# One decoder layer on one core: the attention stage's steps put into another order on four engines

## The chip, the cores and the metric

The kernel runs on one core of a Trainium2 chip. The metric is the device time of that core in microseconds (us), from the start of one execution to its end; a profiled execution also gives the span from the first to the last instruction.

## What is computed

Inputs are `x` and `ctx`, 16 sequences of 128 rows of 128 float32 values. Three sublayers follow each other, each with a residual and a layer norm:

```python
x = _layernorm(x + attention(x))            # 16 heads of 8, rotary q and k, softmax over 128 keys
x = _layernorm(x + cross(x, ctx))           # q, k, v = (. @ Wq + bq); correlation by FFT, mean over
                                            # batch and channels, top 11 lags, softmax, rolled sum of v
x = gamma * norm(x + moe(x)) + beta         # 8 experts, top 2 of a gate, relu(x W1 + b1) W2 + b2
x = _layernorm(x)                           # the layer's own norm behind the last sublayer's
# attention, per sequence: qkv = x @ w_qkv.T; q, k = rope(q), rope(k)
# softmax(q @ k.T * 8 ** -0.5) @ v, then @ w_out.T + b_out
```

The change lies in the first sublayer only. All products are carried to float32 accuracy.

## The kernel before

**The stages.** The attention stage fills the first 103 us or so, a short serial stage finds the lags of the cross attention, and from about 115 us on the experts run until the end. Nothing behind the attention stage's last steps is edited.

**One sequence through the attention stage.** The stage works on the sequences n = 0 to 15 one after the other, in a software pipeline; each sequence passes these steps, each a small helper that waits for its semaphores and issues one or a few instructions on one engine:

- TensorE: `qkv(n)` (L953) projects x and the context. `k_transposes(n)` (L1006) and, for n below 3, `q_transposes(n)` (L1014) turn the stacked pieces. `scores(n, u)` (L968), u = 0 and 1, gives two halves of the scores, from which only row maxima are taken. `maxima_transpose(n)` (L1024) turns the maxima into rows. `scoresT(n, u)` (L985) gives the transposed scores with the maxima already subtracted. `weighted(n, u)` (L1030) multiplies the exponentials by v and by ones. `project(n)` (L1052) is the output projection. `keep_clock(n)` and `keep_clock_late(...)` issue idle matmuls, `fold_cross_query()` two small ones.
- ScalarE: `keep_qkv(n)` (L704) copies the projections out of PSUM. `first_piece(n)` (L708) writes the bf16 high parts of q and k; `second_piece(n)` and `second_copy(n)` (L721, L725) the next parts. `kT_copy(n)` (L729) copies the turned k. `mT_copy(n)` (L741) copies the turned maxima. `softmax_exp(n, u)` (L734) takes the exponentials; the four `w1_high_piece(i)` (L699) prepare the experts' first weights.
- GpSimd (POOL): `rope_products(n)` and `rope_sum(n)` (L428, L440) rotate q and k. `remainder(n)` (L446) and `third_piece(n)` (L453) form what is left behind the first and the second part. `pad_v(n)` (L499), `small_columns(n)` (L509), `inverse_deviation(n)` (L490), later `expand_v(g)` and `w1_low_piece(i)`.
- VectorE (DVE): `maxima(n, u)` (L1381) reduces the scores to row maxima, `pieces_of_maxima(n)` (L459) splits them in two bf16 pieces. `reciprocal(n)` and `divide(n)` (L1392, L1398) normalise. `residual(g)` (L1410) adds the bias to four sequences' rows of x. `residual_sum(n)`, `statistics_of_rows(n)`, `mean_and_variance(n)` and `normal_rows(n)` (L1403, L1418, L1423, L467) are the layer norm. For n below 2 DVE also does the rope steps; `keep_turned()` and `keep_folded()` copy small tiles.
- The DMA queue that SyncE issues (SP) brings the inputs, and for each sequence two kinds of transfer. `spread_maxima(n)` (L343) copies the maxima's rows from `mT` into `qT`, two transfers of 32 KB; `scoresT(n, 0)` waits for both. `q_transpose(n)` (L336), n from 3, is a transposing transfer of q's stack into `qT`; it waits for `second_copy(n)` and `third_piece(n)`, and `scores(n, 0)` and `first_piece(n + 2)` wait for it.

**What sets the order.** The order on each engine is written out by hand, as calls in program order; a step blocks everything behind it on its engine. For the middle of the stage a loop `for k in range(8, 16)` stands on each of the four compute engines (L559, L801, L1161, L1485), so that each pass, here called block k, handles for instance `qkv(k)`, `scores(k - 4, .)` and `scoresT(k - 6, .)`. SP's order is written out as well and is the same all the way: `spread_maxima(n)`, `background_load(n)`, `q_transpose(n + 3)`. The background loads with something in them are n = 4 (512 KB of inputs), 5 (tables) and 6 to 9 (a quarter of w1 each, 256 KB), and 15 (w2).

TensorE's block before the change reads:

```python
for k in range(8, 16):
    scoresT(k - 6, 0)
    scores(k - 4, 0)
    qkv(k)
    project(k - 7)
    scoresT(k - 6, 1)
    scores(k - 4, 1)
    weighted(k - 6, 0)
    weighted(k - 6, 1)
    k_transposes(k - 2)
    maxima_transpose(k - 4)
```

**Buffers that tie the engines together.** There is one `scoreT_pair` in PSUM, so `scoresT(n, 1)` waits for `softmax_exp(n, 0)`; one `score_pair`, so each `scores` waits for the `maxima` in front of it; one `rowmax` and one `mstack`; one bank for `qkv`, one for the turned k, one (`pv_bank`) for `weighted`, which is free when `divide` of the sequence in front is done.

## Time and profile before

| | us |
| --- | --- |
| median of 3 runs | 231.09 (230.35 to 231.51) |
| the profiled execution | 231.02 |
| its span, first to last instruction | 229.2 |
| TensorE busy over the span | 214.5 (94%) |
| VectorE busy | 180.9 (79%) |
| ScalarE busy | 142.5 (62%) |
| GpSimd busy | 111.2 (49%) |
| mean granted clock of TensorE | 0.994 of 2.4 GHz |

All times below count from the start of the span. PE is TensorE's matmuls, PEld its weight loads, ACT ScalarE, POOL GpSimd, SPq the queue that issues DMAs. A matmul row with x8 runs from the start of the first to the modelled end of the last; as they are pipelined, the distance from one row's start to the next one's is what the step costs, and that is how such rows are read here. The same holds for short DVE, ACT and POOL instructions, whose rows overlap by up to 0.1 us.

### The profile page before, as it was taken

The numbers are of one execution on the slowest core, as the hardware profiler recorded it, in microseconds if no ns is written. First come the engines' busy times: TensorE is split into PE (matmuls) and PEld (weight loads), VectorE is DVE, ScalarE is ACT, GpSimd is POOL, SyncE is SP. The second block draws the span as 40 slices with busy tenths as digits, with TensorE's granted clock in tenths as the row PEclk, the third lists the DMA queues.
The fourth block names the chain that finished last, engine by engine and source line by source line (L and its number), as shares of the span: only waits on it lengthen the run. The fifth ranks groups of instructions, "written<-read, shape, count | busy, mean of one in ns | idle before, by whom it ended". The sixth has DMA issues, their size and how long they took to land.

```text
span 229.2 us, 7213 instructions
## 1 busy us (share of the span) xinstructions
PE 214.5 (94%) x2724; PEld 184.1 (80%) x2724; DVE 180.9 (79%) x622; ACT 142.5 (62%) x248; POOL 111.2 (49%) x219
## 2 busy tenths in 40 slices
PE   7989899999999979999999999999999999999970
PEld 7766677787777667778887999789988999889970
DVE  0588999999899899876755779897798868875885
ACT  2487899999999995674489300991029610596112
POOL 5189879999989995513630400252002600040484
PEclk9999999999999999999999999999999999999997
DMA  5951634665655651420000000001000100001001
GB/s 138 286 134 35 106 59 65 158 135 106 149 122 91 43 92 18 127 74 1 3 0 0 3 0 1 0 4 45 4 0 0 46 3 1 0 4 46 1 16 34
DMA packets 32454, 12.32 MB, mean 54 GB/s; under 512 B 19906, under 2 KB 32290, under 8 KB 32418
## 3 DMA queue, kind: packets, MB, share of 16 engines
q1 hardware_dynamic: 31554, 11.48, 24.1%
q8 instruction: 22, 0.36, 0.7%
q10 hardware_dynamic: 864, 0.36, 0.7%
q14 instruction: 14, 0.11, 0.2%
HBM read 6.33 MB, written 1.05 MB: 32 GB/s over the span
## 4 chain that ended last, share of the span: by engine, by line
PE 79%; DMA 7%; DVE 6%; ACT 3%; issue 2%; SPq 1%; DVEq 0%; ACTq 0%
PE bank L1328 13%; PE scoreT_pair L1328 12%; PE score_pair L1298 11%; PE scoreT_pair L1298 8%; PE bank L1042 6%; PE bank L1046 5%; PE bank L965 4%; PE scoreT_pair L997 4%; PE score_pair L981 3%; DMA qT_all<-mT 2%; PE bank L1003 2%; PE bank L1059 2%; DMA early<-in_ctxT 2%; DMA qT_all<-stack 2%; PE scoreT_pair L945 2%
## 5 line engine op out<-in xcount | busy, mean ns | idle before, releaser
L1385 DVE TENSOR_REDUCE rowmax<-score_pair 128x8 f32<-128x1024 f32 x32 | 39.0, 1218 | 4.4 <-PE score_pair L981 3.5
L608 POOL TENSOR_TENSOR ve<-mv,table 128x4 f32<-128x4 f32 (+1 forms) x12 | 3.3, 275 | 78.1 <-DVE mv L1745 60.2
L737 ACT ACTIVATE early<-scoreT_pair 128x1024 f32<-128x1024 f32 x32 | 32.8, 1026 | 6.3 <-PE scoreT_pair L997 6.1
L1328 PE MATMUL bank<-w,early 128*128 128x128 f32 x256 | 30.1, 276 | 0.0
L1328 PE MATMUL scoreT_pair<-w,early 128*128 128x128 f32 x256 | 29.9, 275 | 0.0
L1328 PEld LDWEIGHTS bank<-w,early 128*128 128x128 f32 x256 | 29.5, 192 | 0.3
L1328 PEld LDWEIGHTS scoreT_pair<-w,early 128*128 128x128 f32 x256 | 29.2, 192 | 0.0
L1298 PE MATMUL score_pair<-x2T_part,w_part 128*128 128x512 f32 x108 | 28.4, 398 | 0.0
L880 ACT ACTIVATE early<-score_pair,b 128x512 f32<-128x512 f32 x38 | 25.9, 690 | 3.2 <-PE score_pair L1298 2.6
L1042 PE MATMUL bank<-early,v_pad 128*32 128x128 f32 x512 | 26.5, 279 | 0.4 <-DVE attnT L1401 0.3
L1046 PE MATMUL bank<-early,head_ones 128*32 128x128 f32 x512 | 25.8, 273 | 0.0
L1298 PEld LDWEIGHTS score_pair<-x2T_part,w_part 128*128 128x128 f32 x108 | 19.5, 188 | 5.0 <-ACT early L880 1.4
L1298 PE MATMUL scoreT_pair<-x2T_part,w_part 128*128 128x512 f32 x78 | 19.9, 391 | 0.0
L1396 DVE RECIPROCAL rden<-bank 128x128 f32<-128x128 f32 x16 | 15.3, 955 | 3.6 <-PE bank L1046 3.5
L880 ACT ACTIVATE early<-scoreT_pair,b 128x512 f32<-128x512 f32 x26 | 17.6, 690 | 0.0
L1298 PEld LDWEIGHTS scoreT_pair<-x2T_part,w_part 128*128 128x128 f32 x78 | 14.6, 188 | 3.1
L732 ACT ACTIVATE kT_all<-bank 128x1024 bf16<-128x1024 bf16 x16 | 16.3, 1020 | 0.2 <-PE bank L1003 0.2
L1042 PEld LDWEIGHTS bank<-early,v_pad 128*32 128x32 f32 x512 | 12.8, 109 | 4.5 <-ACT early L737 1.7
L1046 PEld LDWEIGHTS bank<-early,head_ones 128*32 128x32 f32 x512 | 15.4, 110 | 0.0
L1733 DVE SCALAR_TENSOR_TENSOR x_ext<-bank,gate,x_ext 128x128 f32<-128x128 f32 x32 | 11.1, 346 | 4.8 <-PE bank L1328 4.7
L997 PE MATMUL scoreT_pair<-qT_all,kT_all 64*128 64x128 bf16 x256 | 12.7, 218 | 1.8 <-DMA qT_all<-mT 1.1
L1733 DVE SCALAR_TENSOR_TENSOR x_ext<-scoreT_pair,gate,x_ext 128x128 f32<-128x128 f32 x32 | 11.1, 346 | 4.0 <-PE scoreT_pair L1328 3.7
(229 smaller groups left out, 472.3 us busy)
## 6 DMA issues: line engine op xcount, KB each, us to landing
w<-in_w SPq DMA_DIRECT2D x8, 256.0 KB, 3.7
x_ext<-in_x SPq DMA_DIRECT2D x4, 256.0 KB, 5.6
qT_all<-mT SPq DMA_DIRECT2D x32, 32.0 KB, 2.3
early<-in_xT SPq DMA_DIRECT2D x3, 256.0 KB, 4.8
early<-in_ctxT SPq DMA_DIRECT2D x3, 256.0 KB, 5.4
out<-qkv_all SPq DMA_DIRECT2D x3, 256.0 KB, 2.3
table<-in_tables SPq DMA_DIRECT2D x1, 321.0 KB
qT_all<-stack SPq DMA_TRANSPOSE x13, 3.3
```

The costliest lines, as they stand in the source:

```text
L732: act.activation(kT[n % DEEP][:, :, :], turned_slots, ACT.Copy).then_inc(s["k_T"], 1)
L737: act.activation(prob[n % 2][:, 2 * u:2 * u + 2, :, :], scoreT_pair[:, :].rearrange("p (i j s) -> p i j s", i=2, j=QUAD), ACT.Exp, scale=S ...
L880: act.activation(hT[:, c, :], hidden_bank(g, c)[:, :], ACT.Relu, bias=b1[:, c:c + 1])\
L965: pe.matmul(qkv_bank[:, 0:3 * D + XC], xT[:, n, :], wqkv[:, :], start=True, stop=True)
L997: mm = pe.matmul(scoreT_pair[:, (QUAD * side + j) * S:(QUAD * side + j + 1) * S], kT[n % DEEP][rows, 2 * j + u, :], qT[n % DEEP][rows, 2 * ...
L1042: pe.matmul(sum_bank(n)[WIDE * j:WIDE * (j + 1), 0:S], v_pad[n % 2][:, j, i, :], prob[n % 2][:, i, j, :], start=(i == 0), stop=(i == QUAD ...
L1046: mm = pe.matmul(sum_bank(n)[WIDE * j:WIDE * (j + 1), S:2 * S], head_ones[:, i * WIDE:(i + 1) * WIDE], prob[n % 2][:, i, j, :], start=Fals ...
L1298: mm = pe.matmul(hidden_bank(g, c)[:, :], w1_part[:, w, c * P:(c + 1) * P], x2T_part[:, x, :], start=(k == 0), stop=(k == 2))
L1328: mm = pe.matmul(expert_bank[k % 4][:, e4 * D:(e4 + 1) * D], hT[:, f, n * P:(n + 1) * P], w2[:, f, :], start=(c == 0), stop=(c == CH - 1))
L1385: dve.tensor_reduce(rowmax[:, H // 2 * u:H // 2 * (u + 1)], score_pair[:, :].rearrange("p (r t) -> p r t", t=S), AX_X, ALU.max).then_inc(s ...
L1396: dve.reciprocal(rden[:, :], sum_bank(n)[:, S:2 * S]).then_inc(s["rden_ready"], 1)
L1733: dve.scalar_tensor_tensor(total, product, weight, total, ALU.mult, ALU.add).then_inc(s["summed"], 1)
```

## The change

The steps are the same, each is issued once as before, and no helper is edited. What differs is the order of the calls on TensorE, ScalarE, GpSimd and VectorE from about 10 us on. The loops over k are written out. SP's order is not edited.

```diff
             # GpSimd
             rope_sum(pool, 3)
-            pad_v(1)
             third_piece(pool, 2)
             remainder(pool, 3)
             rope_products(pool, 4)
+            third_piece(pool, 3)
             rope_sum(pool, 4)
-            third_piece(pool, 3)
+            small_columns(0)
+            rope_products(pool, 5)
             remainder(pool, 4)
-            rope_products(pool, 5)
             third_piece(pool, 4)
...
-            for k in range(8, 16):
-                rope_sum(pool, k - 1)
-                third_piece(pool, k - 2)
-                small_columns(k - 4)
-                inverse_deviation(k - 8)
-                remainder(pool, k - 1)
-                rope_products(pool, k)
-                pad_v(k - 4)
+            pad_v(5)
+            remainder(pool, 9)
+            small_columns(9)
+            rope_products(pool, 10)
+            pad_v(6)
+            rope_sum(pool, 10)
+            third_piece(pool, 9)
+            inverse_deviation(2)
+            remainder(pool, 10)
...
+            remainder(pool, 11)
+            rope_products(pool, 12)
+            third_piece(pool, 11)
...
+            remainder(pool, 13)
+            rope_products(pool, 14)
+            third_piece(pool, 13)
+            pad_v(10)
+            small_columns(13)
+            rope_sum(pool, 14)
+            remainder(pool, 14)
+            rope_products(pool, 15)
             rope_sum(pool, 15)
             third_piece(pool, 14)
...
+            w1_low_piece(2)
             inverse_deviation(11)
             inverse_deviation(12)
-            pad_v(15)
             inverse_deviation(13)
+            w1_low_piece(3)
             inverse_deviation(14)
             # ScalarE
             first_piece(3)
+            keep_qkv(5)
             mT_copy(0)
-            keep_qkv(5)
+            second_piece(3)
             kT_copy(2)
-            second_piece(3)
             second_copy(3)
+            keep_qkv(6)
             first_piece(4)
             softmax_exp(0, 0)
             mT_copy(1)
             second_piece(4)
-            second_copy(4)
             softmax_exp(0, 1)
             kT_copy(3)
-            keep_qkv(6)
+            second_copy(4)
...
-            for k in range(8, 16):
-                softmax_exp(k - 6, 0)
-                second_piece(k - 2)
-                second_copy(k - 2)
-                softmax_exp(k - 6, 1)
-                kT_copy(k - 3)
-                first_piece(k - 1)
-                keep_qkv(k)
-                mT_copy(k - 4)
...
+            softmax_exp(6, 0)
+            mT_copy(7)
+            second_copy(10)
+            second_piece(10)
+            keep_qkv(12)
+            softmax_exp(6, 1)
+            kT_copy(9)
+            first_piece(11)
...
-            w1_high_piece(0)
-            w1_high_piece(1)
-            w1_high_piece(2)
-            w1_high_piece(3)
             mT_copy(13)
             softmax_exp(12, 0)
             kT_copy(15)
+            w1_high_piece(0)
             softmax_exp(12, 1)
+            w1_high_piece(1)
...
             softmax_exp(14, 0)
+            w1_high_piece(2)
             softmax_exp(14, 1)
             softmax_exp(15, 0)
             softmax_exp(15, 1)
+            w1_high_piece(3)
             # TensorE
             scores(0, 0)
+            fold_cross_query()
             k_transposes(1)
             q_transposes(1)
-            fold_cross_query()
             scores(0, 1)
...
+            k_transposes(3)
+            maxima_transpose(1)
             scoresT(0, 0)
             scores(2, 0)
-            maxima_transpose(1)
-            k_transposes(3)
+            qkv(7)
             scoresT(0, 1)
             scores(2, 1)
             weighted(0, 0)
             weighted(0, 1)
-            k_transposes(4)
             maxima_transpose(2)
             scoresT(1, 0)
             scores(3, 0)
-            qkv(7)
+            k_transposes(4)
             project(0)
             scoresT(1, 1)
             scores(3, 1)
             weighted(1, 0)
             weighted(1, 1)
+            scoresT(2, 0)
+            scores(4, 0)
+            maxima_transpose(3)
             k_transposes(5)
-            maxima_transpose(3)
-            for k in range(8, 16):
...
+            scores(8, 0)
+            scoresT(6, 0)
+            k_transposes(9)
+            maxima_transpose(7)
+            qkv(12)
+            project(5)
+            scoresT(6, 1)
+            scores(8, 1)
+            weighted(6, 0)
+            weighted(6, 1)
...
+            maxima_transpose(11)
             scoresT(10, 0)
             scores(12, 0)
             keep_clock_late(2, qkv_bank, "qkv_kept")
+            k_transposes(13)
...
             # VectorE
             third_piece(dve, 0)
+            keep_turned()
+            remainder(dve, 1)
             residual(0)
-            remainder(dve, 1)
             qT_copy(0)
-            keep_turned()
             third_piece(dve, 1)
...
             maxima(2, 1)
-            residual(2)
             pieces_of_maxima(dve, 2)
             reciprocal(0)
             divide(0)
             maxima(3, 0)
-            residual(3)
+            residual(2)
             residual_sum(0)
             maxima(3, 1)
...
+            maxima(6, 0)
+            normal_rows(dve, 0)
+            residual_sum(3)
+            maxima(6, 1)
+            residual(3)
+            pieces_of_maxima(dve, 6)
+            reciprocal(4)
+            divide(4)
+            maxima(7, 0)
...
```

In TensorE's new order block k opens with `scoresT` and then `scores` for k = 8, 10 and 14, the other way round for k = 9, 11, 12, 13 and 15; `maxima_transpose(k - 5)` and `k_transposes(k - 3)` follow behind these two, and then `qkv(k)` (in block 13 `k_transposes(10)` stands behind `qkv(13)`). On ScalarE `mT_copy(n)` for n = 5 to 10 stands directly behind `softmax_exp(n - 1, 0)`; for n = 3 and 4 it stands in front of `softmax_exp(n - 1, 0)`. The two `second` steps, in either order, and `keep_qkv(k)` then stand in front of `softmax_exp(k - 6, 1)`, with `second_copy` behind it in a few blocks.

## Rows read from the trace of the kernel before

**Rows 1.** Busy time by stretch: per engine us and (instructions), then clock, DMA share, GB/s.

```profile
10.00:20.00 10.00, 9.08 (x101) 7.14 (x99) 8.29 (x16) 7.92 (x16) 7.92 (x14) 1.00 0.55 131
20.00:30.00 10.00, 8.32 (x151) 6.23 (x152) 8.58 (x14) 8.53 (x15) 8.73 (x18) 1.00 0.47 75
...
40.00:50.00 10.00, 10.00 (x223) 7.86 (x223) 9.20 (x21) 9.53 (x17) 9.04 (x21) 1.00 0.70 160
...
80.00:90.00 10.00, 8.56 (x210) 6.58 (x208) 9.07 (x20) 8.18 (x13) 7.44 (x11) 1.00 0.34 60
```

**Rows 2.** The waits of 33.3 to 73.3 us: total us, times, longest.

```profile
DVE rden L1396 <- PE bank L1046: 2.0, 8, 0.3
ACT early L737 <- PE scoreT_pair L997: 1.9, 8, 0.2
```

**Rows 3.** The chain that ended last, 22 to 29 us: start, us, what.

```profile
22.48 0.41 PE scoreT_pair L997 x8
...
22.92 1.02 ACT early L737
...
24.14 0.60 SPq L348
...
24.78 3.53 DMA qT_all<-mT
...
28.35 0.40 PE scoreT_pair L997 x8
```

**Rows 4.** Timeline of TensorE where block 8 begins: start us, us, instruction.

```profile
32.74 0.62 PE L1003 MATMUL bank<-ident,stack 128*128 128x128 bf16 x8
33.20 0.22 PE L1028 MATMUL bank<-ident,mstack 128*128 128x128 bf16 x1
33.35 0.40 PE L997 MATMUL scoreT_pair<-qT_all,kT_all 64*128 64x128 bf16 x8
33.59 0.39 PE L981 MATMUL score_pair<-kT_all,qT_all 48*128 48x128 bf16 x8
33.91 0.93 PE L965 MATMUL bank<-wqkv,early 128*128 128x392 f32 x2
```

**Rows 5.** Timeline of TensorE around `maxima_transpose(1)`.

```profile
22.70 0.41 PE L981 MATMUL score_pair<-kT_all,qT_all 48*128 48x128 bf16 x8
23.04 0.23 PE L1028 MATMUL bank<-ident,mstack 128*128 128x128 bf16 x1
23.11 0.61 PE L1003 MATMUL bank<-ident,stack 128*128 128x128 bf16 x8
```

**Rows 6.** Timeline of ScalarE: `kT_copy(3)`.

```profile
25.51 1.03 ACT L732 ACTIVATE kT_all<-bank 128x1024 bf16<-128x1024 bf16 x1
```

**Rows 7.** `spread_maxima(7)` on SP (53.8 to 55.5 us), its landing; landing of `spread_maxima(5)`.

```profile
53.93 1.25 SPq L348 DMA_DIRECT2D qT_all<-mT  x2
...
DMA to landing us min/median/max: 2.5/2.8/3.1
...
DMA to landing us min/median/max: 2.4/2.6/2.8
```

**Rows 8.** Timeline of VectorE: `residual(2)`.

```profile
26.14 0.72 DVE L1415 TENSOR_TENSOR x_ext<-x_ext,bias 128x512 f32<-128x512 f32 x1
```

**Rows 9.** Timeline of GpSimd: `third_piece(4)`.

```profile
24.56 1.06 POOL L456 TENSOR_TENSOR stack<-rest,stack 128x256 bf16<-128x256 f32 x1
```

**Rows 10.** The tile mstack, whole run: duration ns min/median/max, first and last start.

```profile
L465 DVE TENSOR_TENSOR mstack<-rowmax,mstack x16: 194/197/332, 18.6 to 90.0; 128x16 bf16<-128x16 f32 x16
```

**Rows 11.** Timeline of SP: `q_transpose(4)`.

```profile
25.70 2.01 SPq L341 DMA_TRANSPOSE qT_all<-stack  x1
```

**Rows 12.** The chain that ended last, 77 to 86 us.

```profile
77.16 4.73 DMA qT_all<-stack
...
84.84 1.03 ACT kT_all L732
```

**Rows 13.** Timeline of GpSimd in front of `third_piece(14)`.

```profile
75.46 0.30 POOL L506 COPY v_pad<-qkv_all 128x128 f32<-128x128 f32 x1
```

More of the change, by code:

```diff
@@ new lines, in _ @@
+            first_piece(7)
+            mT_copy(4)
+            softmax_exp(3, 0)
+            second_piece(7)
+            keep_qkv(9)
+            softmax_exp(3, 1)
+            second_copy(7)
+            kT_copy(6)
+            first_piece(8)
+            softmax_exp(4, 0)
+            mT_copy(5)
+            second_copy(8)
+            second_piece(8)
+            keep_qkv(10)
+            softmax_exp(4, 1)
+            kT_copy(7)
+            first_piece(9)
+            softmax_exp(5, 0)
@@ new lines, in _ @@
+            keep_qkv(13)
+            second_copy(11)
+            softmax_exp(7, 1)
+            kT_copy(10)
+            first_piece(12)
+            softmax_exp(8, 0)
+            mT_copy(9)
+            second_copy(12)
+            second_piece(12)
+            keep_qkv(14)
+            softmax_exp(8, 1)
+            kT_copy(11)
+            first_piece(13)
+            softmax_exp(9, 0)
+            mT_copy(10)
+            second_piece(13)
+            second_copy(13)
+            keep_qkv(15)
@@ L1158, in _ @@
             weighted(1, 1)
+            scoresT(2, 0)
+            scores(4, 0)
+            maxima_transpose(3)
             k_transposes(5)
[L1160 to L1171 removed]
+            qkv(8)
@@ new lines, in _ @@
+            project(1)
+            scoresT(2, 1)
+            scores(4, 1)
+            weighted(2, 0)
+            weighted(2, 1)
+            scores(5, 0)
+            scoresT(3, 0)
+            maxima_transpose(4)
+            k_transposes(6)
+            qkv(9)
+            scoresT(3, 1)
+            scores(5, 1)
+            project(2)
+            weighted(3, 0)
+            weighted(3, 1)
+            scoresT(4, 0)
+            scores(6, 0)
+            k_transposes(7)
+            maxima_transpose(5)
@@ new lines, in _ @@
+            qkv(10)
+            project(3)
+            scoresT(4, 1)
+            scores(6, 1)
+            weighted(4, 0)
+            weighted(4, 1)
+            scores(7, 0)
+            scoresT(5, 0)
+            k_transposes(8)
+            maxima_transpose(6)
+            qkv(11)
+            project(4)
+            scoresT(5, 1)
+            scores(7, 1)
+            weighted(5, 0)
+            weighted(5, 1)
+            scores(8, 0)
+            scoresT(6, 0)
+            k_transposes(9)
@@ new lines, in _ @@
+            maxima_transpose(7)
[5 more added lines that the diff above has]
+            weighted(6, 1)
+            scores(9, 0)
+            scoresT(7, 0)
+            maxima_transpose(8)
+            qkv(13)
+            k_transposes(10)
+            project(6)
+            scoresT(7, 1)
+            scores(9, 1)
+            weighted(7, 0)
+            weighted(7, 1)
+            scoresT(8, 0)
+            scores(10, 0)
@@ new lines, in _ @@
+            k_transposes(11)
+            maxima_transpose(9)
+            qkv(14)
+            project(7)
+            scoresT(8, 1)
+            scores(10, 1)
+            weighted(8, 0)
+            weighted(8, 1)
+            scores(11, 0)
+            scoresT(9, 0)
+            k_transposes(12)
+            maxima_transpose(10)
+            qkv(15)
+            project(8)
+            scoresT(9, 1)
+            scores(11, 1)
+            weighted(9, 0)
+            weighted(9, 1)
+            maxima_transpose(11)
```

229 lines of the change are left out of this document (163 added, 66 removed).

## The prediction

> **What bounds the kernel now.** The profiled execution took 231.02 us, 0.07 under the median of 231.09, with a span of 229.2; the sum is made against 231.02. About 0.5% (1.16 us) is what a measurement of this kernel can tell from no change.
>
> The busy times by stretch come first [rows 1]. The reader is to see that TensorE is full from 30 us on (10.00 of 10 us), and not full before (9.08 and 8.32) nor in the drain (8.56): a new order of the same work can win only in the 2.6 us of the two ramp rows, in the drain, or in how fast TensorE gets from one step to the next. Then the waits of the middle [rows 2]: in 8 blocks of 5.0 us VectorE waits 2.0 us and ScalarE 1.9 us in all, some 0.25 us a block each. They follow TensorE closely; cheaper small operations on VectorE buy nothing there by themselves, and an order that costs either more than 0.25 us a block is paid by TensorE. The chain [rows 3] shows what holds the ramp: `scoresT(0, 0)` at 22.48, its exponential at 22.92, behind that `mT_copy(1)`, the spread of the maxima issued at 24.14, and `scoresT(1, 0)` at 28.35 when the second of its two transfers has landed. This is a loop from one sequence to the next, and it took 5.87 us.
>
> **Ramp, 10 to 32 us.** Taken step by step in the new order, each step with the duration of its like.
> (a) `residual(0)` goes behind `remainder(1)`, so the first scores start some 0.4 us earlier; by `mT_copy(0)`, which waits for maxima and a transpose, 0.2 of it is left.
> (b) `third_piece(3)` goes ahead of `rope_sum(4)`: `q_transpose(3)` issues about 1.1 us earlier. `residual(2)`, 0.64 from start to start and 0.72 long [rows 8], leaves the front of `pieces_of_maxima(2)`: `maxima_transpose(2)` is ready some 0.7 us sooner.
> (c) `second_copy(4)` goes behind `softmax_exp(0, 1)` and `kT_copy(3)`. The latter starts at 25.51 and takes 1.03 [rows 6], so the copy ends near 26.75, and `q_transpose(4)`, issued at 25.70 before [rows 11], issues no sooner. SP's order is unchanged, so `spread_maxima(2)` stands behind it and comes about 0.5 later than it could; I find it landing about when it is needed. But `spread_maxima(1)` is then alone on the queue. Before, `q_transpose(4)` was issued 0.3 us behind it, and its second transfer landed 3.53 us after its start [rows 3]; of the later ones the row of `spread_maxima(5)` shows 2.4 and 2.8 [rows 7]. From its first issue on that is 4.17 before and about 2.9 to 3.0 after: `scoresT(1, 0)` moves from 28.35 to about 27.15.
> (d) `qkv(7)` (two matmuls of 0.93 [rows 4], 0.9 with the rest) moves ahead of it into gaps, `k_transposes(4)` (0.46 [rows 4], 33.20 less 32.74) moves behind: 0.44 more is done ahead of the wait.
> (e) Against this, `second_copy(5)` and `second_piece(5)` now wait in front of `softmax_exp(1, 1)` for `remainder(5)`, and `weighted(1, 1)` waits some 0.25 for the exponential.
> From 1.2 + 0.44 less 0.25 and less the 0.1 that `spread_maxima(2)` may cost, I take 1.25: the end of `weighted(1, 1)`, 32.74 before [rows 4], comes at 31.5. Bounds: 0.4, if only (d) holds, and 1.7.
>
> **The blocks, 32 to 73 us.** Same steps, other neighbours. Before, k_transposes, maxima_transpose, scoresT and scores take 33.91 less 32.74, 1.17 us [rows 4]. After, scoresT to scores is 0.24 and k_transposes to the next 0.46 as before, scores to maxima_transpose is 0.34 and from there to k_transposes 0.07 [rows 5]: 1.11. So TensorE alone would win 0.06 a block, 8 x 0.06 = 0.5.
>
> But `mT_copy(n)`, n = 5 to 10, now stands behind `softmax_exp(n - 1, 0)`, because the maxima are turned inside block n + 5 instead of at the end of the block in front. That closes the loop of [rows 3] in the middle: from `scoresT(n - 1, 0)` to the spread's issue 24.14 less 22.48 = 1.66, and 0.05 from landing to `scoresT(n, 0)`, so two of these cannot be closer than 1.71 plus the time from first issue to last landing. That is half of the two transfers' 1.25 on SP, 0.62, plus the landing of the second one: for n = 7 0.62 + 3.1 = 3.7, for n = 5 0.62 + 2.8 = 3.4 [rows 7]; n = 6 and 8 are as n = 5, and 9 and 10 some 0.2 to 0.4 shorter. It is longer than with idle queues because the background loads are issued right behind each spread; they stay there. Before, the copy stood in front of the exponential and a landing had 0.7 to 1.2 us to spare, so this cost nothing; that cover is gone. The spacings become 5.13 to 5.17 (n = 6, 8) and 5.45 (n = 7), where TensorE alone needs 4.95 (4.72 and 5.18 where `scores` and `scoresT` change places). For the six distances from n = 4 to n = 10: 5.18 + 5.17 + 5.48 + 5.12 + 5.18 + 4.80 = 30.93, against 6 x 5.005 = 30.03. The two distances in front stay at 10.0. With `maxima_transpose(11)` (0.1) not counted twice, the blocks cost +0.8 us net of the 0.5. Bounds: -0.5, if no landing is late, and +5.2, if each takes the 5.87 of [rows 3]. `residual(3)` (0.8) now falls into block 10 and delays `maxima(7, 0)` by more than VectorE's spare 0.25; that ends inside the same waits. GpSimd's steps and their queue have the same sum per block and hide beside TensorE.
>
> **VectorE against GpSimd.** `pieces_of_maxima` has an instruction with two SBUF inputs; 16 of them took 194 to 332 ns with a median of 197 [rows 10], although GpSimd is busy nine tenths of the time [rows 1]. There is nothing left to win there. In the ramp a clash is seen: `third_piece(4)` took 1.06 us [rows 9] beside `residual(1)`; the new order leaves this one in place. I cost the rest of the clashes at 0, within 0.3 either way.
> The Trainium skill, page "SBUF — State Buffer", section "SBUF: two separate sides", says that a VectorE operation with two SBUF inputs and a GpSimd operation hold a shared port pair by an exclusive lock, so that the one that comes second blocks until the other has ended. The trace agrees for long operations and not for the small ones.
>
> **Drain, 73 us to the end.** `scores(14, 0)` waits for `q_transpose(14)`, 4.73 us from 77.16 [rows 12], which waited for `third_piece(14)`. One `pad_v`, 0.30 [rows 13], leaves the front of that: -0.25. `kT_copy(15)`, the next gate [rows 12], keeps the same two steps in front. The four `w1_high_piece` (0.55 each) leave that stretch, but were hidden beside the wait for `maxima_transpose(13)`; the last one now stands between the last exponential and ScalarE's table load, where some 0.7 us of slack covers it. `w1_low_piece(3)` goes in front of `inverse_deviation(14)`, with about 1 us to spare. `project` ahead of `scoresT` in the last sequences gives 0.2 and takes it back: 0. Bounds: -0.8 and +0.6.
> Behind 103 us nothing is touched.
>
> **Sum.** 231.02 - 1.25 + 0.8 - 0.25 = 230.3.
>
> **The rivals.**
> (A) The forecast: the ramp's gain is mostly eaten by the landings. 230.3. Chance 0.45.
> (B) The landings are not late: the spreads, issued 1.3 us later in their block, meet less traffic, and take 3.2 or less from first issue. Then 8 blocks give -0.5: 231.02 - 1.25 - 0.5 - 0.25 = 229.0. For it: n = 9 and 10 come near that already. Against: the loads stay right behind the spread. Chance 0.32.
> (C) Slower: the spread meets the next `q_transpose`, as it did in [rows 3]. `third_piece(11)` and `third_piece(13)` now come directly behind the rope products, so `q_transpose(11)` and `(13)` are issued almost together with the end of the spreads of n = 8 and 10. At 5.87 for a distance these two give 0.75 and 1.05 more: 232.1; with one more of them 232.8. It decides from an average of the six issue-to-landing times of 3.7 upward, since (1.5 + 1.16) / 6 = 0.44 above a distance of 5.0 loses the whole gain and 0.5%. Chance 0.10.
> (D) The ramp does not move: a transfer, or `exp(1, 1)`, holds block 8 at its old time less 0.4. Then 230.6 with no late landing and 231.2 with them. Chance 0.10.
> (E) Small VectorE operations are blocked for a whole GpSimd one: a wait of 0.7 in each block, 0.25 of it covered, is 8 x 0.45 = 3.6 in place of the 0.8: 233.1. [rows 10] speaks against it. Chance 0.03. It is the lock of the Trainium skill's page named above, taken at its word.
>
> **How the numbers follow.** Faster by over 0.5% (under 229.86) is most of B and a little of A: 0.35. Slower by over 0.5% (over 232.18) is half of C, E, and a little for what I have missed: 0.11. The rest, 0.54, is within. The range takes in A with its bounds, B, and C's first value: 228.8 to 231.9. A alone would be 229.6 to 231.0.
>
> **What would show it.** Right in the ramp: `scoresT(1, 0)` near 27.2, `weighted(1, 1)` ending near 31.5. Right in the blocks: waits of TensorE's scoresT for the spread, largest (about 0.5) at n = 7, none at n = 9; the distance of `scoresT(n, 0)` equal to 1.71 plus issue to landing. Right in the drain: `scores(14, 0)` still waiting for its transpose. Wrong: no waits for the spread and blocks of 4.95 (B); transposing transfers issued within 0.5 us of a spread's end and landings beyond 4 us (C); `scoresT(1, 0)` after 28 (D); VectorE's small rows above 0.5 us (E).

## The result, and the profile after

The changed kernel took 235.36 us (median of 4 runs, 233.64 to 236.77), the kernel before 231.3 beside it. The ratio is 1.0145, with an interval of 1.0098 to 1.0193: slower by 1.5%, where 230.3 was forecast. The profiled execution took 233.64 with a span of 231.8, that is 2.6 more than before; it was the fastest of the four, and the others are 1 to 3 us longer still. So times of a kernel are compared by medians, and what is read inside a profile explains 2.6 of the 4.1 us between the medians. Single executions far above the rest, such as one of 722.72 us in e1 and one of 271.36 in e9, are left out of all ratios and intervals.

First the busy time by stretch, of the changed kernel (columns as in [rows 1]).

```profile
10.00:20.00 10.00, 8.91 (x100) 6.92 (x98) 8.45 (x16) 8.37 (x18) 8.12 (x14) 1.00 0.54 132
20.00:30.00 10.00, 7.67 (x145) 5.85 (x146) 7.33 (x13) 7.45 (x13) 8.29 (x19) 1.00 0.41 73
...
60.00:70.00 10.00, 9.00 (x212) 7.14 (x210) 9.04 (x17) 8.93 (x16) 7.84 (x18) 1.00 0.41 83
70.00:80.00 10.00, 8.92 (x192) 7.05 (x192) 8.68 (x17) 8.73 (x16) 8.09 (x17) 1.00 0.54 95
80.00:90.00 10.00, 8.85 (x221) 6.81 (x216) 9.46 (x19) 8.49 (x14) 6.21 (x14) 1.00 0.68 70
```

The ramp, in which time was to be won, is emptier than before (7.67 against the 8.32 of [rows 1]), and from 60 to 80 us TensorE lost its full rows (9.00 and 8.92, against 10.00 and 9.66 before). The other engines are less busy in these rows as well. The waits of 33.3 to 73.3 us say for what (columns as in [rows 2]).

```profile
POOL rest L450 <- ACT stack L767: 3.2, 4, 1.6
ACT early L785 <- PE scoreT_pair L1101: 2.4, 5, 0.8
PEld scoreT_pair L1101 <- DMA qT_all<-mT: 1.9, 3, 1.1
...
PE scoreT_pair L1101 <- DMA qT_all<-mT: 1.3, 2, 0.8
```

TensorE waits for the spread of the maxima (3.2 us in five waits), and the same window of before has no such wait. The chain of the changed kernel shows the loop twice, in the ramp and at sequence 8 (start, us, what; to be held against [rows 3]).

```profile
22.97 0.35 PE scoreT_pair L1101 x8
23.34 1.02 ACT early L785
24.56 0.59 SPq L348
25.19 4.06 DMA qT_all<-mT
29.30 0.42 PE scoreT_pair L1101 x8
...
60.64 0.60 SPq L348
61.29 3.43 DMA qT_all<-mT
64.77 0.42 PE scoreT_pair L1101 x8
```

The transfer that took 3.53 us takes 4.06, although the `q_transpose(4)` to which the prediction ascribed its length has gone from behind it: SP's queue in the changed kernel shows it 2.6 us later.

```profile
24.56 1.24 SPq L348 DMA_DIRECT2D qT_all<-mT  x2
27.18 1.25 SPq L341 DMA_TRANSPOSE qT_all<-stack  x1
28.47 1.24 SPq L348 DMA_DIRECT2D qT_all<-mT  x2
```

Below, "spread n" is `spread_maxima(n)`, S(n) the start of `scoresT(n, 0)`, and L(n) the time from the first issue of spread n to its last landing, read from the timelines of TensorE and SP and from the times at which the landings were counted in the trace.

| us | before | after |
| --- | --- | --- |
| S(0) | 22.48 | 22.90 |
| S(1) - S(0) | 5.87 | 6.40 |
| S(4) - S(1) | 15.01 | 13.96 |
| S(10) - S(4) | 30.04 | 32.79 |
| S(15) - S(10) | 21.24 | 21.51 |
| S(15) - S(0) | 72.16 | 74.66 |
| end of the span - S(15) | 134.58 | 134.29 |
| L(1) | 4.17 | 4.70 |
| L(5), (6), (7) | 3.45, 3.46, 3.77 | 3.49, 3.49, 2.78 |
| L(8), (9), (10) | 3.42, 3.21, 3.07 | 4.08, 3.98, 3.89 |

The loss lies between sequences 4 and 10: +2.75 us. S(8) - S(7) is 5.79, S(9) - S(8) 5.69 and S(10) - S(9) 5.60, and each is 1.71 + L(n) to 0.02. This is the loop of the prediction, with an L of 3.9 to 4.1 where it had 3.0 to 3.4.

### The profile page after: what moved, and what is told of

It is laid out like the page before. It is cut to its first block, busy times and chain, and to the rows that moved or that the text cites. A ratio compares the mean times of both kernels' runs of the same rounds, so it can differ in the third digit from the quotient of the medians.

```text
span 231.8 us, 7213 instructions
## 1 busy us (share of the span) xinstructions
PE 214.7 (93%) x2724; PEld 184.7 (80%) x2724; DVE 183.8 (79%) x622; ACT 143.5 (62%) x248; POOL 110.6 (48%) x219
## 4 chain that ended last, share of the span: by engine, by line
PE 62%; DVE 12%; DMA 7%; issue 7%; POOL 5%; ACT 4%; SPq 1%; DVEq 0%; POOLq 0%; ACTq 0%
PE bank L1501 12%; PE scoreT_pair L1501 12%; PE score_pair L1471 11%; PE scoreT_pair L1471 8%; DMA qT_all<-mT 7%; DVE rowmax L1558 4%; PE bank L1146 2%; PE scoreT_pair L1049 2%; PE scoreT_pair L1101 2%; ACT early L785 2%; PE bank L1150 2%; PE bank L1044 1%; SPq L348 1%; POOL qk L444 1%; PE score_pair L1085 1%
```

## The experiments: is it the next transposing transfer?

**e1 and e2.** In both kernels SP holds back `q_transpose(n)` until the spread in front of it has landed:

```diff
                 sp.wait_ge(s["lo"], n + 1)
+                if n > TURNED_Q:
+                    sp.wait_ge(s_m[(n - 3) % DEEP], 32 * landed(n - 3))
```

> The changed kernel, with one edit on SP: q_transpose(n), n from 4, waits until both transfers of spread_maxima(n - 3) have landed. Two theories of where the 2.6 us of the attention stage went. Held back: the transposing transfer, issued while a spread is under way, holds back the last of the 16 completions of the spread's second transfer by 1 to 2 us (n = 1: fifteen by 27.32, the last at 29.25; n = 8: 63.46 and 64.72; n = 10: 74.95 and 76.00). Then every spread takes 2.8 to 3.5 us from its first issue, scoresT(1, 0) comes near 27.5 instead of 29.3, and the kernel is 2.5 to 4 us faster than the changed one: a profiled time of 230 to 231, so within 0.5% of the kernel before. Loop: the latency comes from the order of copy and exponential and from the background loads alone; then the wait only delays the transposes, the late completions stay, and the time is 233 to 236.

> The same edit on SP alone, in the kernel before. Held back: only spread 1 was hit there (26.91 and then 28.30, q_transpose(4) issued at 25.70), and scoresT(1, 0) was the first step of the blocks; it comes 0.5 to 1.3 us earlier and the kernel gains as much, 229.8 to 230.6. In the blocks q_transpose was issued 3.2 us behind the spread, so nothing changes there. Loop: no spread is changed, q_transpose(4) comes later for nothing, the time is 231 to 231.5.

e1, made from the changed kernel, took 236.0 us (ratio to before 1.0203, interval 1.0156 to 1.025). e2, made from the kernel before, took 234.53 (1.0136, 1.0091 to 1.0181). SP's queue in e1:

```profile
24.45 1.24 SPq L350 DMA_DIRECT2D qT_all<-mT  x2
28.45 1.25 SPq L343 DMA_TRANSPOSE qT_all<-stack  x1
```

Spread 1 is alone on its queue until it has landed at 28.36, and L(1) is still 3.91; L(7) to L(10) are 3.96, 3.93, 4.19 and 4.16. So a spread is late without a neighbour on SP's queue, and the prediction's reading of [rows 3] and [rows 11] falls. In e2 spreads 8 to 10, 3.1 to 3.4 before, are 3.79, 4.51 and 4.42, and S(15) - S(0) is 75.81 in place of 72.16: what was thought peculiar to the new order can be had in the old one by shifting things a little. e1 came out as the second of its two theories had it, e2 as neither did, and this was the first hint that it matters where in time a spread falls.

**e3.** The changed kernel with `maxima_transpose(n)`, n = 3 to 10, back at the end of the block in front, and the copy of the maxima back in front of the exponential:

```diff
-            softmax_exp(6, 0)
             mT_copy(7)
+            softmax_exp(6, 0)
...
             weighted(1, 1)
+            maxima_transpose(3)
             scoresT(2, 0)
             scores(4, 0)
-            maxima_transpose(3)
```

> The changed kernel with the closed loop undone: maxima_transpose(n) of n = 3 to 10 back at the end of block n + 4, and mT_copy(n) of n = 5 to 10 in front of softmax_exp(n - 1, 0). Loop theory, and also held-back theory for the part in the blocks: each spread is issued about 1.3 us earlier in its block, so that even a completion held back by 1.3 us arrives in time; the blocks run at 5.0 us or a little under and the 2.6 us lost between scoresT(5, 0) and scoresT(10, 0) come back: 231 to 232 on the profile. The ramp's loss stays (scoresT(1, 0) near 29.3). A rival, that VectorE's or GpSimd's new order holds the blocks (residual(3), statistics behind maxima): then the time stays at 233.5 or more and TensorE waits for maxima or v_pad instead.

It took 233.52 us (1.0112, 1.0078 to 1.0147). The spreads are issued about a microsecond earlier in the block, and from 33.3 to 73.3 us TensorE waits for none of them, not even for spread 5, whose L was 4.89 and which landed 0.22 before S(5). In their place it waits for VectorE, as the waits of 33.3 to 73.3 us of e3 show:

```profile
PEld bank L1132 <- DVE mstack L465: 3.4, 6, 1.1
```

So 1.8 of the 4 us between the medians hang on the closed loop, and its cure brings another wait: in the new order VectorE's pieces of the maxima aren't ready at the block's end.

**e4.** The new order up to `weighted(1, 1)`, the old blocks and the old drain behind it. At the seam `k_transposes(5)` and `maxima_transpose(3)` stand as they did; three small steps (`pad_v(3)`, the statistics of sequence 0, `residual(3)`) had to go where the two orders meet.

```diff
             weighted(1, 1)
-            scoresT(2, 0)
-            scores(4, 0)
-            maxima_transpose(3)
             k_transposes(5)
...
+            maxima_transpose(3)
+            for k in range(8, 16):
+                scoresT(k - 6, 0)
+                scores(k - 4, 0)
```

> The new order on all four engines up to the end of weighted(1, 1), the old one from block 8 on (residual(3) in block 10). My prediction said the ramp gains 1.25 us. By the trace of the changed kernel it does not: scoresT(1, 0) at 29.3 against 28.35, since q_transpose(4) is issued 0.15 us before the spread would have landed and its last completion comes 1.9 us late, while 0.44 us more is done ahead of it. Held back: scoresT(1, 0) again near 29 in the profile, scoresT(2, 0) near the old time, the whole within 0.5 us of the kernel before, with a scatter from run to run of 1 to 2 us as the race falls. If it comes out at 229.8, the ramp was as predicted and the changed profile was an unlucky one.

It took 232.62 us (1.0059, 1.0023 to 1.0096). In its profiled execution S(0) came 2.5 us later than in the changed kernel, with the same calls in front of it. The rows of TensorE say why: until about 10.6 us they are slow, the second projection 1.51 us where the changed kernel has 0.93. The trace's record of the granted clock agrees: its first entry, of 1.00, stands at 10.62 us in e4 and at 4.66 in the changed kernel, and before its first entry the view prints 1.00 without any. So when TensorE comes to its full clock differs between executions with the same work in front, and a total holds this difference. Therefore distances are read: S(15) - S(0) is 71.91, 0.25 under the kernel before, with L(1) at 3.75. By the medians the new ramp costs 1.5 us, which these distances don't show; the larger part of the 4 us is lost in the blocks.

## The experiments: the fetch of TensorE's own instructions

The late spreads of the two kernels and of these four have something in common. A transfer is counted as landed in 16 steps, here called completions, so a spread of two transfers has 32. In the changed kernel's spread 1 the 31st comes at 27.32, 0.05 behind the 30th, and the last at 29.25. And the traffic of the window holds one packet of another queue. Here is the changed kernel from the issue of spread 1, 24.56 to 26.9 us, and from that of spread 8, 60.64 to 62.9 (queue, kind: packets, MB, share of 16 engines).

```profile
q1 hardware_dynamic: 265, 0.06, 19.3%
q8 instruction: 1, 0.02, 2.5%
...
qT_all<-mT SPq DMA_DIRECT2D x2, 32.0 KB, 3.1
```

```profile
q1 hardware_dynamic: 582, 0.14, 34.2%
q8 instruction: 1, 0.02, 2.9%
...
qT_all<-mT SPq DMA_DIRECT2D x2, 32.0 KB, 2.8
```

The queues of the whole run show how rare these are:

```profile
q1 hardware_dynamic: 31554, 11.48, 25.0%
q8 instruction: 22, 0.36, 0.7%
...
q14 instruction: 14, 0.11, 0.2%
```

A q8 packet is 16384 bytes and is under way for 0.9 to 2.0 us. From the first one behind 15 us to the fifteenth the changed kernel's trace has 3616 of TensorE's instructions and the trace of before 3599: one packet for 258 and 257 in the mean, though from one packet to the next it can be 174 or 333 matmuls and weight loads. Of the 14 kernels e9 alone has fewer of TensorE's instructions than before (5540 recorded against 5582), and it alone has 21 such packets and not 22. So the packet is taken to bring TensorE's own program, and is called its fetch below. The Trainium skill, page "Runtime: NRT & Kernel Launch", section "Instruction fetch mechanics", says that each sequencer refills its instruction memory in 16 KB blocks of 256 instructions through a DMA queue of its own while it executes, and that crossing a block is mostly hidden. The sizes agree. Hidden it may be for TensorE itself, as no wait of TensorE is put down to it here; whether it is for others' transfers is tried next.

To test it, the four next kernels change neither the order nor the work behind 23 us. They only make TensorE's stream of instructions in front of S(0) longer, so that its 16 KB boundaries fall elsewhere. The means are the fillers with which TensorE bridges its first 22 us, 7 `stay_busy` and 14 `keep_clock` matmuls of 128 columns in float32, 4 instructions each.

**e5 to e8, small fillers.** 7 fillers become 46 (e5, from the changed kernel), or all 21 become 122 (e6 from the changed kernel, e7 from the kernel before, e8 from e4), of this form, two instructions each (the helper that issues them is written out here):

```diff
-            stay_busy(WARM_UP, mean_w)
+            for _ in range(46):
+                pe.matmul(out_bank[0:32, 0:32], mean_w[:, 0:16].bitcast(BF16), mean_w[:, 0:16].bitcast(BF16), start=True, stop=True)
```

> The changed kernel, in whose first three microseconds 7 float32 fillers on TensorE (28 instructions) give way to 46 small bf16 ones (92): every later instruction of TensorE stands 64 places further on in its queue's stream, and nothing else changes. Theory F (instruction fetch): TensorE's instructions come in transfers of 16 KB, one for some 256 instructions, and the spread whose first 2.4 us meet one waits for a completion 2.1 to 2.6 us after the fetch's start. At 256 instructions in 5.0 to 5.8 us, 64 places are 1.3 us: the fetches stand 1.3 us earlier against the spreads. Spread 1: fetch at +0.9 after the issue in place of +2.3, length 3.2 to 3.4 in place of 4.70; spread 6 at -0.2, spread 7 at +1.1 (3.4 in place of 2.79), spreads 8, 9 and 10 at +0.4 to +0.6, length 3.0 to 3.4 in place of 4.08, 3.99, 3.89. scoresT(10,0) less scoresT(1,0) 44.5 to 45.5 in place of 46.75, the whole 233 to 234. Theory R (what the order itself puts beside the spread: q transposes, background loads): spreads 8 to 10 stay at 3.9 to 4.1, spread 1 at 4.7, spread 7 at 2.8, and the time at 235.4.

> The changed kernel with 160 more instructions in TensorE's stream before spread 0, by small bf16 fillers in the place of float32 ones (66 pairs in the first stage, 56 in place of 14 fillers until 18 us). Theory F: the fetches stand 3.3 us earlier against the spreads, so that none starts in the first 2.4 us of spreads 1 and 6 to 10 (at -1.0, -2.2, -0.9, and -1.4 for the last three): lengths 2.8 to 3.1 for all of these, in place of 4.70, 3.49, 2.79, 4.08, 3.99, 3.89. Then scoresT(1,0) starts 1.5 us earlier against scoresT(0,0) (4.9 us in place of 6.40), the steps from scoresT(6,0) to scoresT(10,0) take 5.0 to 5.2 us in place of 5.24, 5.79, 5.68, 5.60, and the whole comes to 231 to 232. Theory R: lengths and steps as in the changed kernel, 235.4.

> The kernel before with the same 160 more instructions in TensorE's stream. Theory F: of its spreads only the first of the ramp was waited for late (4.16, fetch at +1.7, which goes to -1.6): its length becomes 2.8 and scoresT(1,0) comes 1.2 us earlier against scoresT(0,0) (4.7 us in place of 5.87). The blocks after it stay at 5.00 to 5.01 (their bound is TensorE's work), spreads 5 to 8 drop from 3.4 to 3.8 to 2.8 to 3.1 and only widen the slack, spreads 9 and 10 get a fetch at -0.6 and stay under 3.8. The whole 230.0 to 230.6 in place of 231.1, if no later step takes it back. Theory R: all as before, 231.1.

> The kernel with the new ramp and the old blocks (the run before with that cut) with the same 160 more instructions. Theory F: spread 1 falls from 3.75 to 2.8, scoresT(1,0) comes 0.9 us earlier against scoresT(0,0), the spreads 5 to 8 fall from 3.4 to 4.2 to 2.8 to 3.1; the whole comes down from 232.6 to 231.2 to 231.8, still not under the kernel before with the shift. Theory R: 232.6, lengths as they were.

The times are 234.34 (1.0121, 1.0036 to 1.0206), 238.99 (1.0304, 1.0225 to 1.0384), 235.2 (1.0136, 1.0029 to 1.0244) and 235.54 us (1.0174, 1.0091 to 1.0258). These totals answer another question, since TensorE ran slow for longer. The first projection takes the same 1.6 us in e7 and in e11 (below), whose fillers are full width, but the one behind it doesn't. Timeline of TensorE, e7 first:

```profile
4.05 1.62 PE L964 MATMUL bank<-wqkv,early 128*128 128x384 f32 x2 [1.07 <-DMA early<-in_ctxT]
...
7.86 1.65 PE L970 MATMUL bank<-wqkv,early 128*128 128x392 f32 x2 [0.25 <-ACT qkv_all L706]
```

```profile
4.00 1.59 PE L1068 MATMUL bank<-wqkv,early 128*128 128x384 f32 x2
...
7.37 0.90 PE L1074 MATMUL bank<-wqkv,early 128*128 128x392 f32 x2
```

In e7 the projection still takes 1.62 at 16.95 us and 0.93 at 20.74, and S(0) comes at 27.32 in place of 22.48. The clock record has its first entry at 18.56 in e7, at 18.65 and 18.15 in e6 and e8, and at 6.04 in e11. What TensorE did before was 1.9 us of small fillers and 1.07 us of nothing, then projections with small fillers between them. For e5, whose fillers are small in the first 3 us alone, the first entry at 10.96 proves nothing: e4 and e10, with full-width ones, have it at 10.62 and 10.27.

Inside these runs the spreads can still be read. In e5 the fetch that met spread 1 at +2.3 us stands at -0.5, L(1) is 2.78 in place of 4.70 and S(1) - S(0) 4.48 in place of 6.40. L(8) fell from 4.08 to 2.91, its fetch now at its very issue. L(9) and L(10) stayed at 3.97 and 3.96, and their fetches stayed too, at +1.95 and +1.77, where the expectation had them move. In e6 it is L(7) that grows, 2.78 to 4.19, with a fetch at +1.75. In e7 and e8 L(1) is 2.79 and 2.78, with no fetch from -1.6 to +2.4. In e8 this took S(1) - S(0) from 5.46 to 4.48. In e7 the distance is 6.13 all the same, for the granted clock was 0.50 (1.2 GHz) from 28.80 to 32.22, after TensorE had been idle for 1.39 us in front of S(0), and its rows of eight matmuls took 0.65 in place of 0.40.

**e9 to e12, fillers of full width.** e9, from the changed kernel, takes 21 bf16 fillers of 512 columns (2 instructions each, 42 fewer in all). The others take 84 bf16 fillers of 128 columns, 84 instructions more, and their first ones are shown with the helper written out: e10 in the kernel before, e11 in the changed one, e12 in e4.

```diff
-            stay_busy(WARM_UP, mean_w)
+            for _ in range(28):
+                pe.matmul(out_bank[:, 0:P], mean_w[:, 0:P // 2].bitcast(BF16), mean_w[:, P // 2:P].bitcast(BF16), start=True, stop=True)
```

> The changed kernel with its 21 fillers of the first 22 us made of one bf16 matmul of 512 columns each (2 instructions) in place of a float32 one (4): TensorE's stream is 42 instructions shorter before spread 0, the fillers stay full width and as long as they were. Theory F: the fetches stand 0.9 us later against the spreads, so that they miss the first 2.4 us of spreads 1 (+3.1), 8, 9 and 10 (+2.7) and stay in spread 6 (+2.0). Lengths: spread 1 2.8 in place of 4.70, spreads 8 to 10 2.8 in place of 4.08, 3.99, 3.89, spread 6 3.9 to 4.2 in place of 3.49. scoresT(1,0) less scoresT(0,0) 4.4 to 4.9 in place of 6.40, the steps 8 to 10 5.0 to 5.2 in place of 5.6 to 5.8, scoresT(15,0) less scoresT(0,0) 71.5 to 72.5 in place of 74.66; scoresT(0,0) at 22.9 if the granted clock rises when it did; the whole 232.5 to 233.5. Theory R (the order itself): 74.66 and 235.4.

> The kernel before with 84 more instructions ahead of spread 0, full width: 84 bf16 fillers of 128 columns (2 instructions each) in place of 21 float32 ones. Theory F: the fetches stand 1.75 us earlier. Spread 1: fetch at 0.0, length 2.8 to 3.1 in place of 4.16, scoresT(1,0) 1.0 to 1.2 us earlier against scoresT(0,0). Blocks stay at 5.00. Spread 15 gets a fetch at +0.7 and is waited for up to 1 us longer. The whole 230.2 to 231.1 if the clock rises when it did. Theory R: 231.1, spread 1 at 4.2.

> The changed kernel with the same 84 more instructions. Theory F: fetches 1.75 us earlier: at +0.5 of spread 1, -0.6 of spread 6, about 0 for spreads 8, 9 and 10, +1.0 of spread 15. Lengths: spread 1 2.8 to 3.3 in place of 4.70, spread 6 2.8 to 3.0, spreads 8 to 10 2.8 to 3.3, spread 15 3.2 to 4.1 in place of 2.78. scoresT(1,0) less scoresT(0,0) 4.5 to 5.0, scoresT(15,0) less scoresT(0,0) 71.5 to 72.7 in place of 74.66, the whole 232.5 to 233.5. Theory R: 235.4.

> New ramp, old blocks, and the 84 more instructions: the candidate to beat both. Theory F: spread 1 at 2.8 in place of 3.75 (fetch at 0.0 in place of +1.7), scoresT(1,0) less scoresT(0,0) 4.5 in place of 5.45, blocks at 5.00 to 5.10, scoresT(15,0) less scoresT(0,0) 70.7 to 71.2 in place of 71.90. The whole 231.3 to 232.0 in place of 232.6, about the kernel before. Theory R: 232.6.

| | time, us | ratio to before (interval) | S(1) - S(0) | S(10) - S(4) | S(15) - S(0) |
| --- | --- | --- | --- | --- | --- |
| after | 235.36 | 1.0145 (1.0098 to 1.0193) | 6.40 | 32.79 | 74.66 |
| e9 | 235.31 | 1.0147 (1.0096 to 1.0197) | 5.74 | 33.74 | 76.06 |
| e11 | 231.41 | 1.0025 (0.9985 to 1.0065) | 4.48 | 30.59 | 71.94 |
| before | 230.99 | 1 | 5.87 | 30.04 | 72.16 |
| e10 | 231.41 | 1.0016 (0.9985 to 1.0048) | 5.33 | 30.06 | 71.88 |
| e12 | 231.43 | 1.0037 (1.0004 to 1.0071) | 4.48 | 30.12 | 71.38 |

e11 decides it. With the change's order untouched, 84 more filler instructions took 4 us off the median, of which 2.7 are seen between S(0) and S(15) of the two profiles; the rest lies in executions of which there is no trace. Its chain in the ramp starts as that of the changed kernel did, 0.4 us later, and ends otherwise:

```profile
23.40 0.33 PE scoreT_pair L1106 x8
...
27.81 0.42 PE scoreT_pair L1106 x8
```

SP's queue around spread 1 is the same to 0.01 us when both are counted from the first issue, the next transposing transfer 2.62 behind:

```profile
24.99 1.24 SPq L348 DMA_DIRECT2D qT_all<-mT  x2
27.61 1.25 SPq L341 DMA_TRANSPOSE qT_all<-stack  x1
28.90 1.24 SPq L348 DMA_DIRECT2D qT_all<-mT  x2
```

and what differs is the packet. Traffic of e11 from the issues of its spreads 1 and 8 (24.99 to 27.2, 59.65 to 61.9):

```profile
q1 hardware_dynamic: 238, 0.06, 18.4%
...
qT_all<-mT SPq DMA_DIRECT2D x2, 32.0 KB, 2.2
```

```profile
q1 hardware_dynamic: 785, 0.19, 45.6%
...
qT_all<-mT SPq DMA_DIRECT2D x2, 32.0 KB, 2.2
qT_all<-stack SPq DMA_TRANSPOSE x1, 5.1
```

Spread 8 meets more other traffic than in the changed kernel (785 packets in 2.25 us against 582), has a quarter of w1 and a transposing transfer issued behind it as there, and lands 2.82 us after its first issue instead of 4.08. Spreads 6 and 7, with quarters of w1 behind them too, take 2.79: the background load isn't what makes a spread long. The waits of 33.3 to 73.3 us no longer name the spread; what is left of TensorE's waits is mostly `scores`, for ScalarE's copy and for VectorE's maxima:

```profile
PEld score_pair L1090 <- ACT kT_all L780: 1.0, 4, 0.3
PEld score_pair L1090 <- DVE rowmax L1563: 0.9, 3, 0.4
DVE rowmax L1563 <- PE score_pair L1090: 0.9, 2, 0.5
...
ACT early L785 <- PE scoreT_pair L1106: 0.7, 2, 0.4
```

e9 missed its expectation, and still speaks for the cause. The fetches did not go 0.9 us later. They fell into spreads 1 and 5 to 9, at +1.70, +1.91, +1.73, +2.13, +1.77 and +2.10, and these had 4.05, 3.98, 3.74, 4.20, 4.26 and 4.17 us; spread 10, with a fetch at +2.34, had 2.85. Its waits of 22 to 98 us:

```profile
PEld scoreT_pair L1107 <- DMA qT_all<-mT: 6.4, 7, 1.5
...
PE scoreT_pair L1107 <- DMA qT_all<-mT: 5.1, 7, 1.3
```

The expectation missed in e10 too (L(1) 3.63 where 2.8 to 3.1 was expected, a fetch at +0.3), and neither e10 nor e12 beats the kernel before. So adding instructions moves the fetches, but not by an amount that could be foretold.

All 14 profiles together hold 224 spreads. Sorted by the start of TensorE's fetch after the spread's first issue:

| fetch starts, us after the first issue | spreads | L: median (lowest to highest) |
| --- | --- | --- |
| none from -1.6 to +2.4 | 81 | 2.79 (2.74 to 4.42) |
| -1.6 to -0.8 | 27 | 2.80 (2.75 to 3.51) |
| -0.8 to 0.3 | 23 | 3.09 (2.77 to 4.89) |
| 0.3 to 1.0 | 33 | 3.45 (3.06 to 4.62) |
| 1.0 to 1.5 | 22 | 3.58 (3.35 to 4.22) |
| 1.5 to 2.2 | 30 | 3.98 (3.71 to 4.51) |
| 2.2 to 2.4 | 8 | 2.82 (2.78 to 4.70) |

It isn't the place in the loop that sorts them. Within one n, the undisturbed spreads 1, 6, 7 and 8 of all kernels took at most 2.83, and those in the row from 1.5 to 2.2 at least 3.71; for n = 9 it is 3.22 and 3.82.

In the row from 1.5 to 2.2 the last completion comes 2.0 to 2.5 us after the fetch's start, whatever the kernel. In 24 of these 30 it comes alone, 0.76 to 1.69 behind the other 31, and 1.02 to 1.29 after the end of the q8 packet. It follows that end: in before, e1 to e4 and e9 the fetch of spread 1 starts at +1.69 to +1.71, the packet is under way for 1.37, 1.13, 1.07, 0.98, 1.02 and 1.27 us, and L(1) is 4.17, 3.91, 3.85, 3.71, 3.75 and 4.05, the longer the packet the longer. In the other 6 the last two come together, 0.4 to 1.4 behind the other 30, as they would if one DMA engine were held back in both transfers. From 2.2 on nearly all completions are through. The one late spread of that row is the changed kernel's own spread 1: its fetch starts at +2.26, its last completion comes alone, 1.51 after the packet's end, and none of the other seven shows this, so it is the least certain of the late ones. A spread without a fetch in the window is late in two cases (4.42 in e2, with one at +2.41; 3.84 in e10), so something else can do it as well, seldom.

## Why the prediction was wrong

**The order of reading, right.** TensorE full, the ramp with something to win, the loop from one `scoresT(n, 0)` to the next, and its closing in the blocks because `mT_copy(n)` went behind `softmax_exp(n - 1, 0)`: the runs bear this out. The distance is 1.71 + L(n) in the blocks for n = 6 and 8 to 10, to 0.02.

**Step (c), wrong: it failed both in the cause and in the size.** It laid the 4.17 us of L(1) to `q_transpose(4)` and gave the new ramp 2.9 to 3.0. e1, with that transfer held back, measured 3.91; the changed kernel, which issues it 2.6 us behind the spread, 4.70; e5 to e8, e11 and e12, with the fetch elsewhere, 2.77 to 2.79. So S(1) - S(0) became 6.40 instead of 4.87 (27.15 less a start 0.2 before 22.48). The end of `weighted(1, 1)`, forecast for 31.5 and 32.74 before, came at 33.46, so of the ramp's 1.25 nothing was won. The step itself works once the fetch is out of its way: 4.48 in e5, e6, e8, e11 and e12.

**Step (a), a small loss left out.** `maxima_transpose(1)` moved in front of `scoresT(0, 0)` and waits there for VectorE's pieces, so S(0) came 0.42 later instead of 0.2 earlier. Timeline of TensorE, then of VectorE in front of it:

```profile
22.74 0.23 PE L1132 MATMUL bank<-ident,mstack 128*128 128x128 bf16 x1 [0.24 <-DVE mstack L465]
22.90 0.40 PE L1101 MATMUL scoreT_pair<-qT_all,kT_all 64*128 64x128 bf16 x8
```

```profile
21.83 0.48 DVE L463 CAST mstack<-rowmax 128x16 bf16<-128x16 f32 x1
22.35 0.33 DVE L465 TENSOR_TENSOR mstack<-rowmax,mstack 128x16 bf16<-128x16 f32 x1
```

The two instructions of VectorE have medians of 0.19 and 0.20 over the run, so here they took 0.42 longer, beside GpSimd's `rope_products`. This is a clash of the two engines on the critical chain, where the prediction had costed such clashes at 0 within 0.3.

**The blocks, the term mis-sized.** The working had L at 3.4, 3.7, 3.4 and for n = 9 and 10 some 0.2 to 0.4 less, "longer than with idle queues because the background loads are issued right behind each spread". For n = 6 to 10 the lengths came as 3.49, 2.78, 4.08, 3.98, 3.89, the largest where the smallest were expected, and the reason given is wrong: in e11 spreads 6 to 8 have the same loads behind them and took 2.79 to 2.82. The two of [rows 7], 3.45 and 3.77 by this measure, had a fetch at +0.95 and +1.09; in the new order it starts at +1.87, +1.86 and +1.77 of spreads 8 to 10, which is in the table's slowest row. The six distances took 32.79 instead of 30.93. With 84 instructions more they took 30.59.

**Both orders with the same fillers.** e10 and e11 have the same fillers and 231.41 each, with 71.88 and 71.94 from S(0) to S(15). By this pair the new order itself is worth nothing that can be measured, and the 1.5% of the result is where the packets fell, in an order that had given up its slack: e3, with the slack back in the blocks, lost 1.8 us less. It is one pair: another place of the boundaries could favour either order, and which one a kernel gets by itself is luck, here bad for the new order.

**The rivals.** (C) was nearest in direction, slower by late landings, but its mechanism, the next `q_transpose`, was wrong, and its own condition, an average of 3.7 over n = 5 to 10, wasn't met: the average was 3.62, and the ramp's loss did the rest. (D) gave the ramp's failure. (B), landings of 3.2 or less, is what e11 has at n = 5 to 10 (2.79 to 3.21), and its six distances still took 30.59 and not 6 x 0.06 less than the 30.04 of before; e11's rows above show waits of `scores` for 1.0, 0.9 and 0.4 us in their place, which weren't taken apart further. (E) as a price in each block fell. The small operation of VectorE, [rows 10] before, reads in the changed kernel:

```profile
L465 DVE TENSOR_TENSOR mstack<-rowmax,mstack x16: 194/197/640, 18.1 to 92.9; 128x16 bf16<-128x16 f32 x16
```

Its median is the same 197 ns. But the prediction read too much from the median when it said that the trace doesn't agree with the lock for small operations. The 640 ns stand at 18.10, where a `remainder` of GpSimd had begun 0.08 earlier, and end 0.05 behind it; the two of 331, at 22.35 and 38.30, each end 0.05 to 0.06 behind an instruction of `rope_products` that had begun 0.12 to 0.13 before them. So a small operation does wait where it meets a longer one of GpSimd that is under way; it seldom meets one.

**The drain.** Forecast -0.25, measured +0.27 from S(10) to S(15), with L(11), L(13) and L(14) at 3.31, 3.56 and 3.19. The transposing transfer of `scores(14, 0)` no longer stands in the chain there. e11 took 22.22 over this stretch, 0.98 more than before, with a fetch in spread 12 (L 4.18, +1.74) and one in spread 15 (3.56, +0.66). The order's own part in it wasn't separated.

## What to carry to other kernels

When a small transfer sits on the critical loop, look at its 16 completions one by one and at the instruction queues before blaming its neighbours: one completion late out of 16, with an instruction packet in the window, speaks for a fetch. An order that wins or loses by a per cent must be timed at two or more places of the stream's boundaries, for instance with full-width fillers in front, before the order is credited or blamed; and a loop with less than some 1.2 us to spare for its landing (an estimate, 3.98 less 2.79 of the table) can be hit by the fetches that fall into it, so slack is worth having in front of the step that waits, as the old order had it. Totals also hold the time at which TensorE comes to its full clock, here 4.2 to 10.6 us with fillers of full width, so a difference of a per cent is read from a distance inside the profile as well as from medians.

## What the runs showed of the hardware

A 16 KB instruction packet that starts 1.5 to 2.2 us after the first issue of a two-transfer spread of 64 KB goes with the spread's last one or two completions held back and a spread 1.2 us longer in the median (3.98 against 2.79). The undisturbed second transfer lands 2.1 to 2.2 us after its issue. The Trainium skill, page "DMA: Bandwidth & Descriptors", gives a fixed cost of about 2.0 us for a transfer that GpSimd issues (section "Anatomy of one DMA — SWDGE (gpsimd) path"); the transfers here are issued by SyncE, and their 2.1 is close to it. The same page of the Trainium skill says in "Why a DMA increments its semaphore by 16 and not by 1" that the DMA engines finish independently and only the full 16 mean that all has landed. The 16 completions of the trace agree, and the slowest sets the time. Under "Queues, rings and completion order" the Trainium skill says that each DMA engine takes turns between the queues that it has work for, a packet at a time. That would explain why one completion alone is late and follows the packet's end by 1.02 to 1.29 us, but no run shows which engine carried the packet. So the coincidence and its size are shown, and moving the fetch was shown to remove the delay; how the packet delays the completion is not.

What also stays open is where the boundaries fall. In before, e1 to e4 and e9 the first fetch behind spread 1 starts at +1.69 to +1.71, though e9's stream is 42 instructions shorter than that of the changed kernel, where it starts at +2.26. So a count of instructions alone doesn't set it. It may be tied to a step of TensorE that is released then; that wasn't tried.
